# Layer 0's first steps rearranged: small first projections, dense keys spread by transfers, clears moved behind the norms

## The reference, cut to what matters

```python
x = x + L0_xattn(layernorm(x), ctx)   # 16 heads of 8, 8 batch rows of 128 queries and 128 keys
x = x + L0_ffn(layernorm(x))          # 8 experts, the best one per token: square(relu(x fc)) proj
x = x + L1_xattn(layernorm(x), ctx)   # the same form as layer 0, with other weights
x = x + L1_ffn(layernorm(x))          # 8 experts, two per token, gelu

def xattn(x, y):                      # x (8,128,128), y (8,128,96)
    q = x @ Wq.T + bq
    k, v = split(y @ Wkv.T + bkv)
    att = softmax(q k / sqrt(8))      # per batch row and head, over the 128 keys
    return (att @ v) @ Wo.T + bo
```

## Time and profile before

| | before |
|---|---|
| median of three runs | 239.88 us |
| the profiled execution's own time | 240.54 us |
| its span, first to last instruction | 238.8 us |
| TensorE, VectorE, ScalarE, GpSimd busy | 93%, 69%, 51%, 34% |
| mean granted TensorE clock | 0.999 |

### The profile page before, as it was taken

One profiled execution on the slowest core, in us unless ns is written; L12 is line 12 of the kernel. 1 busy time (PEld: TensorE's weight loads), 2 busy tenths in 40 slices (PEclk: granted clock), 3 DMA queues, 4 the chain that ended last, 5 costly groups with the idle time before them and its releaser, 6 DMA issues.

```text
span 238.8 us, 6733 instructions
## 1 busy us (share of the span) xinstructions
PE 221.9 (93%) x2534; PEld 171.7 (72%) x2534; DVE 165.3 (69%) x513; ACT 121.7 (51%) x231; POOL 80.2 (34%) x105
## 2 busy tenths in 40 slices
PE   8899988999999999999988689999799999999993
PEld 8446766776755999999886364877567786776773
DVE  1697666866455685558646765977858974799994
ACT  2555366655476556666630267656645266343340
POOL 8493300001052067756532494764800100000000
PEclk9999999999999999999999999999999999999999
DMA  6990241224004011612030310131300000001001
GB/s 204 376 406 32 72 107 53 62 80 141 3 29 134 5 34 57 168 48 77 25 77 27 90 40 9 52 90 51 92 0 4 0 0 0 3 0 47 3 0 44
DMA packets 12451, 16.38 MB, mean 69 GB/s; under 512 B 1428, under 2 KB 9620, under 8 KB 12292
## 3 DMA queue, kind: packets, MB, share of 16 engines
q1 hardware_dynamic: 10068, 12.87, 17.4%
q0 software_dynamic: 1152, 2.24, 3.2%
q10 hardware_dynamic: 1200, 0.85, 1.1%
HBM read 11.31 MB, written 3.95 MB: 64 GB/s over the span
## 4 chain that ended last, share of the span: by engine, by line
PE 75%; DVE 13%; DMA 5%; issue 3%; POOL 1%; ACT 1%; DVEq 0%; SPq 0%; ACTq 0%
PE ps L1309 12%; PE ps L1297 12%; PE ps L1088 11%; PE ps L1377 7%; PE ps L1387 7%; PE ps L997 6%; PE ps L1145 6%; DVE mx L697 4%; PE ps L1096 3%; DMA wa<-in_wa 2%; PE ps L1017 2%; DVE xn L679 2%; PE ps L1011 2%; PE ps L1053 2%; PE ps L1183 2%
## 5 line engine op out<-in xcount | busy, mean ns | idle before, releaser
L697 DVE TENSOR_REDUCE mx<-ps 128x4 f32<-128x512 f32 x64 | 41.0, 685 | 16.1 <-PE ps L1088 16.1
L522 ACT ACTIVATE PT<-ps 128x512 f32<-128x512 f32 x64 | 35.6, 590 | 24.6 <-PE ps L1096 24.6
L1088 PEld LDWEIGHTS ps<-k,q 32*128 32x128 f32 x512 | 30.9, 186 | 15.3 <-DVE mx L697 11.9
L1088 PE MATMUL ps<-k,q 32*128 32x128 f32 x512 | 36.4, 283 | 5.9 <-DVE mx L697 5.2
L1096 PE MATMUL ps<-q,k 32*128 32x128 f32 x512 | 34.9, 283 | 0.0
L1309 PEld LDWEIGHTS ps<-proj,work 128*128 128x128 f32 x256 | 30.7, 192 | 5.7 <-issue 5.7
L643 ACT ACTIVATE work<-ps,fc 128x512 f32<-128x512 f32 x32 | 21.4, 687 | 24.0 <-PE ps L1297 22.5
L1309 PE MATMUL ps<-proj,work 128*128 128x128 f32 x256 | 31.1, 275 | 0.0
L1096 PEld LDWEIGHTS ps<-q,k 32*128 32x128 f32 x512 | 29.2, 186 | 1.5 <-issue 1.3
L407 POOL DMA_INDIRECT moe_y<-ys,tok_i x22 | 22.3, 1012 | 23.6 <-DVE ys L923 11.5
L1297 PE MATMUL ps<-xT,fc 128*128 128x512 f32 x64 | 30.1, 593 | 0.0
(11 more groups left out here) (156 smaller groups left out, 316.6 us busy)
## 6 DMA issues: line engine op xcount, KB each, us to landing
proj<-in_proj SPq DMA_DIRECT2D x1, 2048.0 KB, 12.8
fc<-in_fc SPq DMA_DIRECT2D x8, 256.0 KB, 3.8
slots_x<-xs SPq DMA_DIRECT2D x2, 709.5 KB, 13.1
fc<-in_w SPq DMA_DIRECT2D x8, 129.0 KB, 2.3
proj<-in_w SPq DMA_DIRECT2D x8, 128.0 KB, 2.5
wr<-in_wr SPq DMA_DIRECT2D x1, 913.0 KB, 8.5
xs<-slots_x SPq DMA_DIRECT2D x2, 322.5 KB, 3.9
xs<-slots_x SPq DMA_DIRECT2D x2, 258.0 KB, 3.0
```

What stands on the lines that cost most here:

```text
L522: nc.scalar.activation(PT[:, j % PTR, :], ps[:, ST_BANK(layer, j), :], ACT.Exp, scale=SCALE).then_inc(b_done, 1)
L697: nc.vector.tensor_reduce(mx[:, b, 4 * g:4 * g + 4], ps[:, S_BANK(layer, j), :].rearrange("p (k m) -> p k m", m=M), axis=AX, op=ALU.max).t ...
L1088: ins = mm(ps[:, S_BANK(layer, 2 * n + i), P * k:P * k + P], q4[r:r + 32, k, L * b:L * b + L], k4[r:r + 32, k, M * b:M * b + M], start=Tru ...
```

## The change

Layer 0's keys and queries of rows 0-1 are projected first, 256 columns wide, in the spread form. Keys of rows 2-3 and rows 4-7 are made dense (`wkd`) in steps 0 and 1, evicted by ScalarE into `k_dense` (a part of `work`), and spread by two sets of four SyncE transfers into `k4`, which ScalarE has filled with the constant beforehand. Queries of rows 2-3 are made in steps 2 and 3 in the spread form; the transpose of rows 4-7 and the values of rows 4-7 move to step 4, the dense queries of rows 4-7 to step 5, the values of rows 0-3 to step 6. Statistics are taken over 2 and 6 rows in place of 4 and 4, and the norms are split into pairs of rows between the maxima. GpSimd's clears wait for the last norm, and the clear of `q4` comes first. `proj` is loaded by expert along with `fc`; the empty slots are written behind rows 2 and 3. The context sum moves into the expert loop, the key bias of layer 1 to step 3. Layer 0's idle products are gone.

```diff
-A_COLS = dict(wk=512, wv=128, bk=4, bv=1, bq=4, wq=512, wqd=128, bqd=1)
+A_COLS = dict(wk=512, wkd=128, bk=4, bkd=1, bq=4, wq=512, wqd=128, bqd=1, wv=128, bv=1)
...
+        FIRST_K_BANK, K_DENSE_BANK = [0, 1, 2, 3], (4, 5)
+        FIRST_T_BANK, FIRST_Q_BANK, Q_MORE_BANK = 4, [5, 6, 7, 3], [4, 3, 5, 6]
+        K_DONE, Q_DONE = (4, 6), (9, 10)
-        V_BANK = [[5, 6], [7, 6]]
+        V_BANK = [[6, 5], [7, 6]]
...  SyncE
-            sp.dma_start(proj[:], proj_in).then_inc(s_fc, 16)
+            def keys_in(part, lo, hi):
+                for g in range(4):
+                    sp.dma_start(k4[32 * g:32 * g + DH, :, lo:hi],
+                                 k_dense[32 * g:32 * g + 32, lo - 256:hi - 256]).then_inc(k_in[part], 16)
             def shift_rows(layer):
                 for b in range(B):
                     sp.wait_ge(m_sb, BB(layer, b))
                     sp.dma_start(q4[DH:P:32, :, L * b:L * b + L], mT[:, b % TRR, :]).then_inc(t_row[b % TRR], 16)
+                    if layer == 0 and b == 0:
+                        sp.wait_ge(k_sb, 6)
+                        keys_in(1, 512, 1024)
...
                     if layer == 0:
                         sp.dma_start(fc[:, b, :], fc_in[:, b, :]).then_inc(s_fc, 16)
+                        sp.dma_start(proj[:, b], proj_in[:, b]).then_inc(s_fc, 16)
+                    if layer == 0 and b in (2, 3):
+                        empty_slots(b - 2)
...
+            sp.wait_ge(k_fill, 1)
+            sp.wait_ge(k_sb, 5)
+            keys_in(0, 256, 512)
             shift_rows(0)
...  GpSimd
             rsqrt(0, 0)
             rsqrt(0, 1)
+            pool.wait_ge(ln_norm, 2)
+            nc.gpsimd.memset(q4[:, :, 512:1024], 0.0).then_inc(q_fill, 1)
             nc.gpsimd.memset(vaug[:], 0.0).then_inc(v_clear, 1)
             pool.wait_ge(v_clear, 1)
             va = vaug[:].rearrange("p b (c j g) x -> p (b c) j g x", c=2, j=2)
             for j in range(2):
                 nc.gpsimd.memset(va[:, :, j, :, 16 + j:17 + j], 1.0).then_inc(v_clear, 1)
-            nc.gpsimd.memset(q4[:, :, 512:1024], 0.0).then_inc(q_fill, 1)
+            pool.wait_ge(q_fill, 1)
+            pool.wait_ge(q_sb, Q_DONE[0])
+            for g in range(4):
+                pool.dma_start(q4[32 * g:32 * g + DH, :, 512:1024], q_dense[32 * g:32 * g + 32, 1, :]).then_inc(q_in[0], 16)
             nc.gpsimd.memset(zero_rows[:], 0.0).then_inc(zero_rdy, 1)
             add_bo(0, 0)
             add_bo(0, 1)
-            pool.wait_ge(q_fill, 1)
-            pool.wait_ge(q_sb, 5)
-            for g in range(4):
-                pool.dma_start(q4[32 * g:32 * g + DH, :, 512:1024], q_dense[32 * g:32 * g + 32, 1, :]).then_inc(q_in[0], 16)
...  ScalarE
+            act.wait_ge(shift_rdy, 1)
+            nc.scalar.activation(k4[:, :, 256:1024], shift_row[:, 0:1].unsqueeze(2).to_broadcast([P, 4, N - 256]), ACT.Copy,
+                                 scale=-1.0).then_inc(k_fill, 1)
...
+                    if layer == 0 and n == 0:
+                        dense_keys_evac(0, 256, 512)
+                    if layer == 0 and n == 1:
+                        more_ln_evac()
+                        dense_keys_evac(1, 512, 1024)
+                    if layer == 0 and n in (2, 3):
+                        queries_evac(1, 2 * n - 4)
+                        queries_evac(1, 2 * n - 3)
+                    if layer == 0 and n == 4:
                         ln_evac(0, 1)
+                    if layer == 0 and n == 5:
                         second_queries_evac()
...  VectorE, behind the maxima of step n
-                    if layer == 0 and n == 1:
-                        context_sums()
-                    if layer == 0 and n in (2, 3):
-                        v_evac(n - 2)
+                    if layer == 0 and n in (0, 1, 2):
+                        first_normalise(2 * n + 2, 2 * n + 4, (ln_norm, None, ln_norm)[n])
+                    if layer == 0 and n == 3:
+                        second_key_bias()
+                    if layer == 0 and n == 4:
+                        v_evac(1)
+                    if layer == 0 and n == 6:
+                        v_evac(0)
...  TensorE, second_half
                 if layer == 0 and n == 0:
+                    dense_keys(0, 256, 512)
+                if layer == 0 and n == 1:
+                    pe.wait_ge(ln_norm, 1)
+                    for i in range(2):
+                        ins = nc.tensor.transpose(ps[:, LN_BANK[0][0], 128 * i:128 * i + 128], xn[:, 2 + i, 0:D], ident[:])
+                    ins.then_inc(ln_tr, 1)
+                    pe.wait_ge(s_ctx[1], 16)
+                    dense_keys(1, 512, 1024)
+                if layer == 0 and n == 2:
                     pe.wait_ge(ln_xT, 1)
                     pe.wait_ge(k_sb, 5)
+                    queries(1, 0)
+                    queries(1, 1)
+                if layer == 0 and n == 3:
+                    pe.wait_ge(k_sb, 6)
+                    queries(1, 2)
+                    queries(1, 3)
+                if layer == 0 and n == 4:
+                    pe.wait_ge(q_sb, 8)
                     ln_transpose(0, 1)
+                    v_proj(0, 1)
+                if layer == 0 and n == 5:
+                    pe.wait_ge(ln_xT, 2)
+                    dense_queries(0)
+                if layer == 0 and n == 6:
+                    pe.wait_ge(q_sb, Q_DONE[0])
                     v_proj(0, 0)
...  TensorE, scores(n) and scores_t(m)
+                    if layer == 0 and n == 4:
+                        pe.wait_ge(k_in[0], 64)
+                        pe.wait_ge(q_sb, 8)
+                    if layer == 0 and n == 8:
+                        pe.wait_ge(k_in[1], 64)
+                        pe.wait_ge(q_in[0], 64)
...
-                    if m == 0 and layer == 0:
-                        pe.wait_ge(q_sb, 5)
+                    if m == 1 and layer == 0:
                         pe.wait_ge(v_sb, 1)
...
-                    if n in (4, 5):
-                        pe.wait_ge(v_sb, 2)
+                    if layer == 1 and n in (4, 5):
                         idle_product(256)
...  TensorE, the start
-            for i in range(3):
-                k_proj(0, i)
+            for k in range(4):
+                first_keys(k)
             pe.wait_ge(pool_const, 1)
-            ln_transpose(0, 0)
-            k_proj(0, 3)
+            pe.wait_ge(first_norm, 1)
+            for i in range(2):
+                ins = nc.tensor.transpose(ps[:, FIRST_T_BANK, 128 * i:128 * i + 128], xn[:, i, 0:D], ident[:])
+            ins.then_inc(first_tr, 1)
             pe.wait_ge(s_wq, 16)
+            pe.wait_ge(first_xT, 1)
             for i in range(3):
-                q_proj(0, i)
+                queries(0, i)
```

More of the change, by code:

```diff
@@ L164, in build @@
         q_dense = work[:, 0:1024].rearrange("p (h n) -> p h n", h=2)
+        k_dense = work[:, 1024:1792]
         yg = work2[:, 1024:2048].rearrange("p (b d) -> p b d", d=D)
@@ L274, in _, with empty_slots @@
             sp.dma_start(wr[:], wr_in).then_inc(s_wr, 16)
-            sp.dma_start(proj[:], proj_in).then_inc(s_fc, 16)
-            sp.wait_ge(pool_const, CONSTS)
-            sp.wait_ge(tok_base, 1)
-            for h in range(2):
+            def empty_slots(h):
+                sp.wait_ge(pool_const, CONSTS)
+                sp.wait_ge(tok_base, 1)
                 sp.dma_start(slots_x[h].rearrange("(p t) d -> p t d", p=P),
@@ L369, in rsqrt @@
                 pool.wait_ge(ln_var, 2 * k + half + 1)
-                sl = slice(4 * half, 4 * half + 4)
+                sl = slice(4 * half, 4 * half + 4) if k else slice(6 * half and 2, 2 + 6 * half)
                 nc.gpsimd.tensor_tensor(rstd[:, sl], ve[:, sl], minus_half[:, sl], ALU.pow).then_inc(ln_rstd, 1)
@@ L661, in ln_stats @@
             def ln_stats(k, half):
-                bs = range(4 * half, 4 * half + 4)
-                sl = slice(4 * half, 4 * half + 4)
+                sl = slice(4 * half, 4 * half + 4) if k else slice(6 * half and 2, 2 + 6 * half)
+                bs = range(sl.start, sl.stop)
                 for b in bs:
@@ L681, in ln_normalise, with first_normalise @@
                 ins.then_inc(ln_norm, 1)
+            def first_normalise(lo, hi, done):
+                dve.wait_ge(ln_rstd, 1 if hi <= 2 else 2)
+                for b in range(lo, hi):
+                    ins = nc.vector.tensor_scalar(xn[:, b, 0:D], xr[:, b, :], mv[:, b, 0:1], rstd[:, b:b + 1],
+                                                  ALU.subtract, ALU.mult)
+                if done is not None:
+                    ins.then_inc(done, 1)
             def v_evac(half):
-                dve.wait_ge(v_ps, half + 1)
+                dve.wait_ge(v_ps, 2 - half)
                 dve.wait_ge(v_clear, 3)
@@ L898, in _ @@
             dve.wait_ge(pool_const, 1)
-            link(nc.vector.tensor_reduce(shift_row[:], ident[:, DH:P:32], axis=AX, op=ALU.add))
```

(13 more changed lines are left out.)

164 lines of the change are left out of this document (85 added, 79 removed).

## The result

The changed kernel takes 244.18 us (median of 4 runs, 243.14 to 246.66) against 239.91: ratio 1.018, 95% interval 1.0142 to 1.0219. It is slower by 4.3 us. 241.7 was forecast, with 1.84 us of loss. The sign was right, the size under half of the loss.

A forecast was written before the change was run, and what follows sets the result against it. TensorE holds 75% of the chain of waits, and time was taken to follow step 8's start: 36.95 against 35.11, 1.84 slower, other terms hidden or 0. 239.88 + 1.84 = 241.7 us, range 239.6 to 244.2.

The forecast's parts named there:

- The order of the waits: Layer 0: clears behind the norms delay v_evac, then step 5, the dense queries and their transfer, then step 8; 1.84 us slower.
- step 5: Loop pass of layer 0, scoring half a batch row; waits for v_evac, start forecast at 26.35 against 29.02 before.
- step 8: Loop pass of layer 0, first to read queries of rows 4-7; start forecast at 36.95 against 35.11 before.
- clears over: GpSimd's clears of q4 and vaug behind the norms of rows 6-7, forecast from 19.7 to 25.4.
- first issue: GpSimd's first transfer of the dense queries of rows 4-7, behind their eviction, forecast at 30.1.
- end of step 7's work: TensorE done with step 7 of layer 0 at 32.95, then standing 4.0 us for the transfer.
- granted clock 1.00 throughout: TensorE's clock was to stay at 1.00 (2.4 GHz) throughout, despite rests of 2.3 at step 5 and 4.0 before step 8.
- rival 1: TensorE's clock falls during the stand before step 8, 1.7 us more over two steps, time 243.4; chance 0.20.
- The way of the transfer: Dense queries of rows 4-7, first issue to last landing: 6.35 as before plus 0.4 for SP's loads alongside.
- The start: First keys on TensorE at 7.27, when the first weights land, as in the kernel before.
- The context sum: VectorE's sum of 1.20 moved from step 1 to tile 5 of the expert loop: 0 to 0.3, taken as 0.
- Rival 3: VectorE's key bias in step 3 waits for the clear of vaug until 25.1: 0.85 more, 242.6; chance 0.07.

The follow-up runs named there:

- e2: Changed kernel without the four transfers of the dense queries of rows 4-7, step 8 waiting for the clear alone: 238.72 us, ratio 0.9933 to the kernel before.
- e10: Changed kernel with the dense queries of rows 4-7 in step 4, their transpose in step 3, values of rows 4-7 in step 5: ratio 0.9917 to the kernel before.
- e1: Changed kernel with idle products where TensorE stands, two ahead of step 5's wait and three ahead of step 8's: ratio 1.0162 to the kernel before.
- e5: Changed kernel with SyncE's loads of row 2 (fc, proj, first empty slots) moved to rows 3 to 5: ratio 1.0173 to the kernel before.
- e9: e5 with idle products that fill the stands, two ahead of step 5 and four ahead of step 8: ratio 1.0027 to the kernel before.
- e7: Kernel before with one edit, the context sum in tile 5 of the expert loop instead of step 1: ratio 1.0008 to the kernel before.
- e8: Changed kernel with proj in one load and both empty-slot writes back ahead of the attention, row 2 loading fc alone: ratio 1.013 to the kernel before.
- e14: Repeat of e7, the kernel before with the context sum alone moved to tile 5 of the expert loop: ratio 1.0007 to the kernel before.
- e4: Changed kernel with the context sum back in step 1 instead of tile 5 of the expert loop: 245.22 us, ratio 1.0196 to the kernel before.
- e12: e10 with the loads of rows 1 and 2 sent from row 3 on, context sum left in tile 5 of the expert loop: 236.93 us, ratio 0.9871.
- e13: e10 with the loads of rows 1 and 2 sent from row 3 on and the context sum in step 7: 236.87 us against 240.15, ratio 0.9886.
- e3: Changed kernel with GpSimd's clears back ahead of the norms of rows 2-7, vaug first, then q4: 244.68 us, ratio 1.0158 to the kernel before.
- e6: Changed kernel with the four transfers of the dense queries issued by SyncE behind row 1's loads instead of by GpSimd: ratio 1.013 to the kernel before.

## Why the prediction was wrong in size

- **The order of the waits was right.** The clears behind the norms hold v_evac, v_evac holds step 5, the dense queries stand behind it, and their transfer holds step 8. Forecast and measured: clears over 25.4 and 23.6, step 5 26.35 and 24.55, first issue 30.1 and 29.17, end of step 7's work 32.95 and 32.7, step 8 36.95 and 36.42. e2 shows that this one wait carries it, and e10 that the order of the products is the cause: the clears behind the norms do no harm once nothing of step 5 waits for v_evac.
- **The step that failed is "granted clock 1.00 throughout".** It was named as rival 1, with a chance of 0.20 and 1.7 us, and left out of the sum. Its price was larger and fell in two places. After the 2.0 us stand of step 5 the clock was down in steps 5 and 6: the dense product took 2.00 for 1.0, and from step 5 to the first issue it was 4.62 us where 3.75 was counted, 0.9 more. In e1 and e5, at full clock, it was 3.69 and 3.70. After the 3.7 us stand steps 8 and 9 took 6.60 in place of 4.37, 2.2 more; e9 against e5 shows that by taking it away.
- **The argument against that rival did not hold.** I leaned on having no row of a fall inside the kernel. The kernel before has no stand over 1.6 us between its products, so its trace could not show one. The measured time lies at the upper edge of the range, which was that rival with 0.8 of company.
- **The way of the transfer** was taken as 6.75 and took 7.16; 6.05 alone (e5).
- **The start** came 1.46 earlier, by scatter as far as e7, e8 and e14 show, and hid the first fall: step 8 lost 1.3, not 1.84. That step 8 came within 0.53 of the forecast is luck: 1.8 early at step 5, against 0.87 from the fall and 0.4 from the transfer.
- **The context sum** was taken at 0 of 0 to 0.3; the tiles lose 0.3 with it (e4, e12 against e13), the total shows nothing of it.
- **Rival 3** (the key bias held by the clear of vaug) did not happen, though the wait behind it exists. The bias started at 19.45, beside q4's clear, and ended with it:

```profile
19.45 0.32 DVE L862 TENSOR_SCALAR bk<-wr,shift_row 128x4 f32<-128x4 f32 x1
```

The clear ran from 17.94 to 19.74. In e4 the same bias took 0.55 us, from 19.80 to 20.35, and ended with a clear that ran from 18.51 to 20.31; in e3, with no clear beside it, 0.22. The Trainium skill (SBUF — State Buffer, SBUF: two separate sides) describes an exclusive lock on the port pair that VectorE and GpSimd share, held for a whole instruction; these rows and e3's norms agree with it.

The sum: 1.31 at step 8, 2.23 in steps 8 and 9, 0.3 in tiles 0 to 12, and 0.3 further on that no run explains: 4.1, the span's difference.

## What to carry to other kernels

When an edit leaves TensorE standing, price the stand twice: the wait, and the slower clock of the work behind it, which here made 2.2 of the 4.1 us lost behind the second stand alone. If a first stand feeds the chain that ends a second one, the first fall lengthens that chain too. Before moving a projection that a transfer must still spread, count back from the step that reads it; 6 us of transfer wanted three steps, and making the product one step earlier turned a loss of 1.8% into a gain of 0.8%, of 1.1 to 1.7% with the loads beside it held back.

## What was not expected of the hardware

TensorE's clock fell behind stands well under the 3.6 us of rest that the prediction read from the earlier trace rows: 2.0 us ahead of step 5 in the changed kernel and in e2, 1.78 ahead of step 8 in e10. It is not sure to: e5 had 2.01 ahead of step 5 and stayed at 1.00, and two later stands of the changed kernel, of 1.5 us each, were followed by no fall. In e12 one of 1.67 us, which ended at 129.53, was:

```profile
129.50:130.00 0.50, 0.47 (x9) 0.35 (x13) 0.50 (x3) 0.15 (x1) 0.00 (x0) 1.00 0.00 0
131.00:132.00 1.00, 1.00 (x6) 0.35 (x6) 1.00 (x2) 0.98 (x2) 0.95 (x1) 0.50 0.09 20
```

What decides it no run shows, nor how long the lower clock meets the work behind it: from step 5 to the first issue it was 3.7 us without a fall (e1, e5, e8), 4.62 in the changed kernel and 5.24 in e4. Three products of 0.94 us inside a stand of 5.3 us did not prevent the fall (e1), while four that filled it did (e9).

A set of four transfers of 64 KB within the chip's SBUF took 6.05 us alone and 7.2 to 8.0 beside 1.2 MB of SyncE's loads. Issued from SyncE's queue it brought no gain, and it held up the shift row behind it (e6).
